# Constants filled during a sort's counting, answer pairs loaded during a sum, one product instead of two at the entry

## The reference, cut to what matters

```
xn = layernorm(x)
embeds = xn @ W_P_w + W_P_b + W_pos                   # 6250 x 128: E
q, k, v = embeds @ q1, embeds @ k1, embeds @ v1       # first attention layer: qs and kv
...
agg = segment_sum(h[src] * alpha, dst) + b_gat        # 16 values a node, by the second graph
scores = layernorm(agg, gamma, beta).reshape(M, 4, 4).mean(1)
g = softmax over the two best of four scores, 0 for the others
out = x + sum over e of g[e] * (gelu(x @ W1[e] + b1[e]) @ W2[e] + b2[e])
```

## Time and profile before

| | us |
|---|---|
| median of three runs | 7081.17 (7080.81 to 7087.0) |
| profiled execution | 7074.46 |
| its span, first to last instruction | 7072.6 |

### The profile page before, as it was taken

One profiled execution on the slowest core, in us unless ns is written; L12 is line 12 of the kernel. 1 busy time (PEld: TensorE's weight loads), 2 busy tenths in 40 slices (PEclk: granted clock), 3 DMA queues, 4 the chain that ended last, 5 costly groups with the idle time before them and its releaser, 6 DMA issues. The chain is left out here.

```text
span 7072.6 us, 118162 instructions
## 1 busy us (share of the span) xinstructions
PE 5305.6 (75%) x28073; PEld 4149.9 (59%) x28073; DVE 5250.9 (74%) x15782; ACT 3459.6 (49%) x9814; POOL 4748.6 (67%) x5326
## 2 busy tenths in 40 slices
PE   5995677777777776667666676666679999999781
PEld 2664555566666665456665665665456666666671
DVE  7994677688888888577777777777667777777776
ACT  0002667666666665566666666665322222222561
POOL 1441777777777775677777777776377777777781
PEclk7557899877777777887777878777578888888555
DMA  1005444444444443454545445444423222322437
GB/s 29 4 4 137 139 140 140 139 130 129 131 129 130 130 131 108 127 138 132 138 131 137 132 132 138 132 132 118 103 49 65 59 59 60 60 63 58 127 120 193
DMA packets 502729, 769.54 MB, mean 109 GB/s; under 512 B 119802, under 2 KB 365657, under 8 KB 502061
## 3 DMA queue, kind: packets, MB, share of 16 engines
q0 software_dynamic: 198048, 441.63, 23.9%
q1 hardware_dynamic: 292961, 308.36, 16.0%
q10 hardware_dynamic: 11052, 12.00, 0.7%
HBM read 689.74 MB, written 71.83 MB: 108 GB/s over the span
## 5 line engine op out<-in xcount | busy, mean ns | idle before, releaser
L706 POOL DMA_INDIRECT att_kv_e<-kv,gnn_idx x3240 | 3108.9, 960 | 1131.9 <-issue 929.7
L791 PE MATMUL att_ps_sum<-att_vals,att_hot 128*125 128x136 f32 x6480 | 1237.0, 347 | 902.9 <-DVE att_vals L849 900.5
L791 PEld LDWEIGHTS att_ps_sum<-att_vals,att_hot 128*125 128x125 f32 x6480 | 1062.4, 238 | 1104.0 <-DVE att_vals L849 1080.5
L777 PE MATMUL att_ps_q<-qs,att_hot_t 125*128 x6480 | 1178.3, 340 | 265.6 <-ACT att_hot_t L823 260.2
L706 POOL DMA_INDIRECT max_rows<-rows,gat_idx x1128 | 1066.0, 945 | 421.1 <-issue 339.4
L777 PEld LDWEIGHTS att_ps_q<-qs,att_hot_t 125*128 125x128 f32 x6480 | 1064.9, 248 | 356.9 <-issue 355.3
L870 DVE TENSOR_TENSOR acc<-acc,att_ps_sum 125x136 f32 x3240 | 938.3, 290 | 265.8 <-DVE acc L870 174.3
L836 DVE TENSOR_TENSOR att_prod<-att_ps_q,att_kv_e 128x512 f32<-128x512 f32 x810 | 556.6, 687 | 764.1 <-issue 432.5
L808 ACT ACTIVATE att_hot<-node_no,gnn_loc 128x125 f32<-128x125 f32 x3240 | 1014.4, 384 | 0.0
L2437 DVE CUSTOM_DVE_ANT_0 max_junk<-max_far,max_ps_b 125x256 bf16<-125x256 bf16 x2256 | 792.4, 416 | 260.8 <-PE max_ps_b L2401 260.8
L801 ACT ACTIVATE att_ps_dve<-att_clipped 128x32 f32<-128x32 f32 x810 | 161.4, 199 | 1396.8 <-DVE att_clipped L857 1395.6
(11 more groups left out here) (454 smaller groups left out, 7971.0 us busy)
## 6 DMA issues: line engine op xcount, KB each, us to landing
att_local<-gnn_loc_rows SPq DMA_DIRECT2D x810, 128.0 KB
att_kv_e<-kv,gnn_idx POOLq DMA_INDIRECT x3240
max_local<-gat_loc_rows SPq DMA_DIRECT2D x282, 128.0 KB
gs_local<-gat_loc_rows SPq DMA_DIRECT2D x141, 256.0 KB, 3.3
outs<-ex_y SPq DMA_DIRECT2D x25, 896.0 KB
max_rows<-rows,gat_idx POOLq DMA_INDIRECT x1128, 2.4
X<-in_x SPq DMA_DIRECT2D x10, 1120.0 KB
ans_late<-outs SPq DMA_DIRECT2D x11, 896.0 KB
```

Source lines behind the costliest of these rows:

```text
L706: pool.indirect_dma_start(rows(j, e), None, source, bass.IndirectOffsetOnAxis(ap=g.idx[:, t:t + 1], axis=0))\
L777: ins = pe.matmul(ps_q[j % 2][:, e * D:(e + 1) * D], hot_t[:, j % 2, e * LANES:(e + 1) * LANES], at(qs, numbers.of(k * GROUP + e)), start= ...
L791: ins = pe.matmul(sum_of(u, i), hot[:, g_of % SLOTS, e, :], vals[:, g_of % VALS, e, :], start=True, stop=True)
```

## The change

It has three parts.

At the start, the first block is gone. `constants` only allocates; `fill_constants` holds the instructions. `sort_constants` fills only `bucket_no` and `pick`, and `fill_marks` holds the rest. Both are issued by GpSimd at the beginning of its list in `sort_edges`, followed by `s.zeros` and one increment of `marks`, for which SP waits before it clears the tables, VectorE and TensorE before the sums over groups.

In `enter` the product with `xT` as weights is gone. TensorE transposes ET back into the plain embedding (`turn_back`, behind `project`), and ScalarE instead of VectorE copies it to E. `ps_t`, `ps_p` and the new `ps_back` have two banks each, and the waits for a bank reach one tile further back. The two broadcast loads of the bias and the instruction that added them are gone.

The answer's slots 4 to 11 lie in `src_sb`, in the part that steps have read; SP loads them in `neighbour_sum`, ten steps after the last read. `gates` loads only slots 12 to 15, all on SP.

```diff
 def sort_constants(...):
             count(s.bucket_no[:], [[1, BUCKETS], [0, WIDTH]])
-            count(s.low_no[:], [[1, LANES], [0, BLOCK]])
...
             chain(pool.memset(s.pick[:], 0.0))
             chain(pool.memset(s.pick[:, GROUPS - 1:GROUPS], 1.0))
...
+def fill_marks(s, pool, chain):
+    count(s.low_no[:], [[1, LANES], [0, BLOCK]])
+    count(s.slot_no[:], [[1, SLOTS_F], [0, BLOCK]], base=OWN // LANES)
...
 def sort_edges(nc, c, s, g):
+            sp.wait_ge(m["marks"], 1)
             sp.dma_start(g.table.rearrange("(p q l) -> p q l", p=LANES, l=LANES),
...
+            dve.wait_ge(m["marks"], 1)
             dve.wait_ge(m["sums"], 1)
...
+            pe.wait_ge(m["marks"], 1)
             pe.wait_ge(m["sums_in"], 1)
...
         @block.gpsimd
         def _(pool):
+            chain = Chain(pool, m["fill"])
+            fill_marks(s, pool, chain)
+            fill_constants(c, pool, chain)
+            pool.memset(s.zeros[:], 0.0).then_inc(m["marks"], 1)
...
 def enter(...):
-        ps_e = psum("ps_e")
-        ps_t, ps_p = (st.enter_context(nc.psum_tensor(f"enter_{n}", [LANES, 512], F32)) for n in ("ps_t", "ps_p"))
+        ps_e, ps_back, ps_t, ps_p = psum("ps_e"), psum("ps_back"), psum("ps_t"), psum("ps_p")
...
             def turn(t, h):
                 pe.wait_ge(m["normed"], t + 1)
-                wait(pe, m["turned_sb"], t)
+                wait(pe, m["turned_sb"], t - 1)
...
             def times_w(t, h):
                 pe.wait_ge(m["turned_sb"], t + 1)
-                wait(pe, m["e_out"], t - 1)
                 wait(pe, m["et_out"], t - 1)
                 for ch in range(KC):
-                    pe.matmul(et_ps(h), wp[:, ch, :], xT[:, t % TURNED, ch, :], start=ch == 0, stop=ch == KC - 1)
-                for ch in range(KC):
-                    ins = pe.matmul(e_ps(h), xT[:, t % TURNED, ch, :], wp[:, ch, :], start=ch == 0, stop=ch == KC - 1)
+                    ins = pe.matmul(et_ps(h), wp[:, ch, :], xT[:, t % TURNED, ch, :], start=ch == 0, stop=ch == KC - 1)
...
             def project(t, h):
-                wait(pe, m["kv_copied"], t)
+                wait(pe, m["kv_copied"], t - 1)
...
+            def turn_back(t, h):
+                pe.wait_ge(m["et_out"], t + 1)
+                wait(pe, m["e_out"], t - 1)
+                pe.transpose(e_ps(h), ET[:, h, :], c.ident[:]).then_inc(m["turned_back"], 1)
...
                 if 0 <= n - 1 < tiles:
                     project(n - 1, (n - 1) % 2)
+                    turn_back(n - 1, (n - 1) % 2)
...
+            def e_out(t, h):
+                act.wait_ge(m["turned_back"], t + 1)
+                act.copy(E[:, t], e_ps(h)).then_inc(m["e_out"], 1)
...
 def neighbour_sum(...):
                 if k % 16 == 15 and k // 16 < EARLY:
                     ans.load(sp, k // 16)
+                for i in range(USED):
+                    if k == min(ans.read(i) + 10, total - 1):
+                        sp.wait_ge(m["weighted"], ans.read(i))
+                        ans.load(sp, EARLY + i)
...
 def gates(...):
-            for p in range(EARLY, HELD, 2):
+            for p in range(EARLY + USED, HELD):
                 ans.load(sp, p)
         @block.scalar
         def _(act):
-            for p in range(EARLY + 1, HELD, 2):
-                ans.load(act, p)
...
-EARLY, HELD = 4, 16
+EARLY, USED, HELD = 4, 8, 16
...
+    def read(i):
+        return -(-(i + 1) * 2 * ALL // (WIDE * (FE + FH)))
```

More of the change, by code:

```diff
@@ L116, in constants @@
     c.pick_head = sb("pick_head", [SPLIT * FH, FH, NODE_TILE], BF16)
[L117 to L144, removed]
@@ L149 @@
+SORT_SEMS = ["fill", "marks", "edges_in", "steps", "one_hots", "counted", "sums_in", "sums", "turn_in", "turned", "dests_in", "dests",
              "tile_ready", "digits_out", "cleared", "tiles_out", "bases_out", "ranked", "reduced", "low", "low16",
@@ L204, in _ @@
[L204 to L218, removed]
-    return s
+    return s
+def fill_marks(s, pool, chain):
+    def count(out, pattern, base=0, by=0):
+        chain(pool.iota(out, pattern, base=base, channel_multiplier=by, allow_small_or_imprecise_dtypes=True))
+    count(s.low_no[:], [[1, LANES], [0, BLOCK]])
+    count(s.slot_no[:], [[1, SLOTS_F], [0, BLOCK]], base=OWN // LANES)
+    count(s.row_no[:], [[1, SPANS * LANES]])
+    count(s.row_start[:], [[RUN * LANES, SPANS]], by=RUN)
+    count(s.pair_no[:], [[1, s.pair_no.shape[1]]])
+    count(s.every_pair[:], [[1, s.every_pair.shape[1]]])
+    chain(pool.memset(s.ones16[:], 1.0))
+    chain(pool.memset(s.rank[:], 1.0))
+    chain(pool.affine_select(out=s.rank[:], in_=s.rank[:], compare_op=ALU.is_ge, fill=0.0, base=0,
+                             pattern=[[1, LANES]], channel_multiplier=-1))
+    chain(pool.affine_select(out=s.rank[:], in_=s.rank[:], compare_op=ALU.not_equal, fill=float(OWN), base=0,
+                             pattern=[[-1, LANES]], channel_multiplier=1))
+    for row, weight in ((NODE_TILE, 64.0), (NODE_TILE + 1, 1.0)):
+        chain(pool.affine_select(out=s.rank[:], in_=s.rank[:], compare_op=ALU.not_equal, fill=weight, base=-row,
+                                 pattern=[[0, LANES]], channel_multiplier=1))
+    pairs_of = [[-2, GROUPS // 2], [0, 2]]
+    def keep(mask, rule, pattern, base, by):
+        chain(pool.affine_select(out=mask[:], in_=mask[:], compare_op=rule, fill=0.0, base=base,
+                                 pattern=pattern, channel_multiplier=by))
+    for mask in (s.same, s.before, s.prev):
+        chain(pool.memset(mask[:], 1.0))
+    keep(s.same, ALU.is_ge, pairs_of, 0, 1)
+    keep(s.same, ALU.is_ge, [[2, GROUPS // 2], [0, 2]], 1, -1)
+    keep(s.before, ALU.is_gt, [[2, GROUPS // 2], [0, 2]], 0, -1)
+    keep(s.prev, ALU.is_equal, pairs_of, 0, 1)
+    keep(s.prev, ALU.is_equal, [[1, GROUPS]], -1, -1)
@@ L3019, in program @@
                 router_weights(nc, c, row, a_dst, best, node_info, gacc)
-                ans = Answer(nc, ctx, x_rows, outs, tiles)
+                ans = Answer(nc, ctx, x_rows, outs, tiles, src_sb)
                 neighbour_sum(nc, c, gat, src_sb, node_info, gacc, ans)
-            ans.more(gs)
-            gates(nc, c, ins, gacc, gate, ans)
-            answer(nc, ans, gate, out)
+                ans.more(edges)
+                gates(nc, c, ins, gacc, gate, ans)
+                answer(nc, ans, gate, out)
 def kernel(**inputs):
```

79 lines of the change are left out of this document (45 added, 34 removed).

## The result

The kernel after takes 7020.89 us (median, 7017.80 to 7028.77) against 7080.99: a ratio of 0.9918, 95% interval 0.9906 to 0.9930, 60 us less where 51 were forecast. Its profiled execution has a span of 7016.1, 56.5 less than before's, and the answer starts 56.56 earlier than in the earlier trace rows. From there on VectorE multiplies and adds without a stall, as before.

What follows compares the result with a forecast made beforehand. The answer's multiply-adds on VectorE set the end, so the prediction shortened the stages before it: -9.4 - 12 - 32.6 + 3 = -51 us, taking the median from 7081.17 to 7030, range 7010 to 7052.

Steps and rivals of the forecast that it cites:

- forecast 9.4: Start, constants beside the first sort's counting: VectorE starts 17.7 us earlier, less 8.3 of waits; bounds 4 and 17.7.
- 2 us of waits for the instructions of tensor_scalar kind: Start of counting: seven such VectorE instructions wait out GpSimd's `slot_no` and shorter fills, about 2 us.
- 14 instructions and 6.5 us in all: Counting at the start: GpSimd's reading fills, affine_selects and one cast, that meet VectorE's comparisons; 6.3 us more waits taken.
- The turns: Counting at the start: VectorE and GpSimd alternate, each waited out once by the other; 6.3 us of waits.
- rival B: Start: VectorE never waits for GpSimd's fills, `group_sum` at 74, time 7022; chance 0.08.
- forecast 12: `enter`: 11.2 us gained by a tile period of 1.56, plus under 1 at the start for broadcast rows; bounds 0 and 20.
- the forecast was 74.2: `enter`, tile 4 to 49: 45 periods of 1.56 plus 4 for statistics, against 85.4 us before; 11.2 gained.
- Rival C: `enter`: stores of k and v bound the stage, period 1.70, gain 5 plus 1, time 7036; chance 0.10.
- Rival E: `enter`: TensorE's clock falls to 1.2 GHz, 47 more tiles cold, 73 us lost, time 7103; chance 0.05.
- forecast 32.6 less 3: `gates`: waits of 26.7 and 7.4 go except 1.5, 32.6 us gained; eight loads moved to `neighbour_sum` cost 3.
- rival D: `gates` and `neighbour_sum`: the 7.4 parameter wait stays and each of eight moved loads costs 0.7, time 7039; chance 0.07.
- the forecast's own sign: Whole kernel: the forecast is wrong if the answer stalls on a pair or an unchanged stage moves more than a few us.

Runs made afterwards that it cites:

- f_wide: The kernel after plus eight GpSimd affine_selects over 128x2000 f16 beside the first sort's counting; `group_sum` at 93.8 us, median ratio to before 0.9936.

## Why the prediction held, and where its sizes were off

**Part 1: forecast 9.4, measured 14.7 in the kernel after and 14.2 alone.** The start was forecast at 8.4 with 2 us of waits for the instructions of tensor_scalar kind; the lists landed at 9.94, 9.1 behind the request and not 7.3, and those waits were 0.6 (0.46 at the first, 0.18 at the cast behind it): together 15.6 earlier, where the forecast had 15.7. That agreement is luck, two errors that cancel. The term that was mis-sized is the next: "14 instructions and 6.5 us in all. If VectorE and GpSimd take turns and each is waited out once, that is 6.3 more". The turns exist (`f_wide`), so rival B, no waits, comes nearest in time (`group_sum` at 76.6, where B said 74 and the forecast 82) with the wrong mechanism; but I took the lengths of rows for the time in which GpSimd keeps VectorE out. It cost 1.0. The Trainium skill's rule on the shared port ("SBUF — State Buffer", section "Who interferes with whom") agrees with `f_wide`, 1.9 us for each select; only with the rows' lengths put into it does it give the 6.3 that did not come.

**Part 2: forecast 12, measured 18.2 in the stage, 16.8 in the median alone.** The mechanism is the forecast one: TensorE itself sets the period, with no wait for the copy in a clean tile. Between tile 4 and 49 the forecast was 74.2, the trace shows 69.5: product 0.45 and not 0.52, turning back 0.11 and not 0.18, 6.3 less in 45 tiles, while statistics and stores took 5.6 and not 4. The other 2.4 of the gain are in the first tiles, for which the forecast had under 1. I costed the second banks at nothing beyond freeing the copy; the projection's was worth about 5, and without it the period is 1.60, more than the forecast's 1.56. Rival C, stores, is there with 5.4 us of ScalarE's waits, but did not set the period. Rival E did not come: the granted clock over the stage is 0.96 as before, and 1.00 from tile 4 on. So here two banks at each hand-over did not let the clock fall: what the Trainium skill ("TensorE: Matmul & The Clock Gate", section "A second HAM failure mode: psum-queue depth-cycling") reports of another kernel did not appear. Of the gain about 2 us come back at the first attention: 46.7 on average in the eight kernels with part 2 and SP's old order (44.9 to 48.5), 44.9 in the four without (44.6 to 45.2). In the kernel after it was 3.1.

**Part 3: forecast 32.6 less 3, measured 31.4 less nothing in its two stages, 23.2 in the median alone.** In `gates` 2.2 of the parameters' wait stayed and 0.4 of the square root's, where 1.5 was left for both. VectorE's waits for `local` did not grow (1.1 us). The gain in the stage is sure: without part 3 it takes 54.6 to 60.6 us in four kernels, with it 27.2 or 27.3 in nine. Neither step of rival D shows: the 7.4 fell to 2.2, and the loads cost the sum nothing. That the median gained 23 only is in no term of the forecast; where the rest went is open (see above).

**The sum.** By stage, before to after: 14.4 up to `enter`'s first product, 18.2 in `enter`, 2.2 in the sum, 31.4 in `gates`, and 9.7 lost where nothing was changed: 56.5, the difference of the two spans. (The medians differ by 60, since before's profiled execution lies 6.5 below its median and after's 3.1.) The 5 and the 6 that parts 1 and 2 brought above the forecast were in part taken by that stretch, so the total lies nearer to the forecast than its parts do, and that is luck. By the forecast's own sign, a stage with unchanged code that moves by more than a few us, it was wrong there: it put that stretch at nothing, and 9.7 and 4.4 were measured in two executions.

## What to carry to other kernels

When constants move beside VectorE's work, price each by its columns, not by the length of its row, and keep only the wide ones out of the way. When a stage gets a product less, look for the single bank whose copy becomes the next wait: taken alone it shows nothing, behind the first edit it is a quarter of the gain. And read the first microseconds after a stage that got faster: a queue's order may be what starts the next one. Here it was so before the change, too (14.82 us for the load of weights), and turning it round in the kernel after was worth 11 us.

## What was not expected of the hardware

- A GpSimd select delays a two-input VectorE instruction by 0.04 us at 128 columns, 0.37 at 500 and 1.9 at 2000, while the row of a 128-column one is 0.29 long alone and 1.14 beside comparisons, of which only the last 0.16 lie behind the comparison that it waited for.
- Iotas do not delay a comparison (1.20 beside two of them, at 12.63), but a tensor_scalar waits one out: it ended at 11.39 whether it began at 9.04 or at 9.94 (11.38 or 11.39 in ten kernels).
- One DMA of weights took 19.46 us to issue behind the clearing of two tables and beside gathers (14.82 in the kernel before), and 0.43 ahead of the clearing.
